# Self-attention in a decoder kernel: each value product cut into two halves of 256 columns, spread over its step

## What is computed

```python
# layer 0: 16 heads of width 16, causal
p = softmax(mask(q @ k.T * scale));  o = p @ v
# layer 1: 32 score heads of width 8; each pair of them shares one 16-wide value head
attn1 = softmax(q1 @ k1.T * scale) @ v12
attn2 = softmax(q2 @ k2.T * scale) @ v12
a = attn1 - lam * attn2          # then a root mean square norm and the output projection
```

## Time and profile before

| | |
|---|---|
| median of three runs | 4204.82 us (4199.30 to 4217.71) |
| profiled execution, its own time | 4222.62 us |
| its span, first to last instruction | 4220.9 us |
| TensorE busy | 3494.9 us (83%) |
| VectorE busy | 2918.8 us (69%) |
| ScalarE busy | 1941.5 us (46%) |
| GpSimd busy | 764.9 us (18%) |
| mean granted TensorE clock | 0.894 of 2.4 GHz |
| products (line 717) | 5632 records, 732.7 us busy, mean 593 ns |
| scores (line 701) | 2816 matmuls, 993.2 us busy |
| scores for the maxima (line 742) | 2816 matmuls, 1004.9 us busy |
| reductions (line 632) | 1408, 1561.4 us busy, 319.1 us idle before them |
| exponentials (line 569) | 2816, 1388.5 us busy, 567.7 us idle before them |

### The profile page before, as it was taken

The page is one execution under the profiler, slowest core; times in us unless marked ns, Lnnn a source line. Parts: engine busy times, 40 slices in busy tenths (PEclk is TensorE's granted clock), DMA queues, the critical chain, the costliest instruction groups (busy, mean ns, idle before and its releaser), DMA issues. The chain is left out here.

```text
span 4220.9 us, 54217 instructions
## 1 busy us (share of the span) xinstructions
PE 3494.9 (83%) x19000; PEld 1704.3 (40%) x19000; DVE 2918.8 (69%) x4353; ACT 1941.5 (46%) x3763; POOL 764.9 (18%) x1063
## 2 busy tenths in 40 slices
PE   7599999766479885999999999999865769999758
PEld 4244443433234452333333333333342434554625
DVE  6566665345546677888888888888645457776374
ACT  2166666222110031777777777777741213334121
POOL 3222222123300041000000000000022433445000
PEclk9689989688779995999999999999987879999678
DMA  5312210000010061000000000000001231110202
GB/s 201 111 44 50 48 44 20 18 35 10 0 41 10 10 198 53 17 24 17 17 24 16 23 18 17 24 16 17 9 3 38 98 104 42 32 32 1 88 17 71
DMA packets 81072, 175.16 MB, mean 41 GB/s; under 512 B 21592, under 2 KB 39008, under 8 KB 79424
## 3 DMA queue, kind: packets, MB, share of 16 engines
q1 hardware_dynamic: 79968, 165.76, 13.0%
q10 hardware_dynamic: 864, 6.29, 0.4%
HBM read 87.76 MB, written 54.72 MB: 34 GB/s over the span
## 5 line engine op out<-in xcount | busy, mean ns | idle before, releaser
L632 DVE TENSOR_REDUCE L_attn_tops<-L_attn_psM 128x2 f32<-128x1024 f32 (+3 forms) x1408 | 1561.4, 1148 | 319.1 <-PE L_attn_psM L742 315.7
L569 ACT ACTIVATE L_attn_E<-L_attn_psS 128x512 f32<-128x512 f32 (+3 forms) x2816 | 1388.5, 576 | 567.7 <-PE L_attn_psS L701 564.1
L701 PE MATMUL L_attn_psS<-L_attn_Q,L_attn_K 64*128 64x512 f32 (+3 forms) x2816 | 993.2, 437 | 126.1 <-ACT L_attn_E L569 101.8
L742 PE MATMUL L_attn_psM<-L_attn_K,L_attn_Q 62*128 62x512 f32 (+3 forms) x2816 | 1004.9, 479 | 55.8 <-DMA L_attn_K<-parts_k 30.3
L701 PEld LDWEIGHTS L_attn_psS<-L_attn_Q,L_attn_K 64*128 64x128 f32 x2816 | 470.1, 192 | 815.7 <-ACT L_attn_E L569 648.4
L717 PE MATMUL L_attn_psO<-L_attn_E,L_attn_V 128*32 128x512 f32 (+3 forms) x5632 | 732.7, 593 | 0.0
L742 PEld LDWEIGHTS L_attn_psM<-L_attn_K,L_attn_Q 62*128 62x128 f32 x2816 | 437.2, 193 | 149.2 <-issue 43.1
L527 POOL TENSOR_TENSOR L_AO<-L_attn_o 128x128 f32<-128x128 f32 x64 | 29.4, 459 | 1446.1 <-DVE L_attn_o L665 1446.1
L1437 PE MATMUL m_psE<-m_we,m_xT 128*128 128x512 f32 x512 | 236.9, 623 | 0.0
L536 POOL TENSOR_SCALAR_AFFINE_SELECT L_attn_E<-L_attn_E 128x128 f32<-128x128 f32 x512 | 146.2, 292 | 463.0 <-ACT L_attn_E L569 451.7
L2135 ACT ACTIVATE x_E<-x_psS 128x512 f32<-128x512 f32 x256 | 138.9, 595 | 179.8 <-PE x_psS L2258 167.1
(11 more groups left out here) (339 smaller groups left out, 3793.1 us busy)
## 6 DMA issues: line engine op xcount, KB each, us to landing
parts_q<-L_proj_parts SPq DMA_DIRECT2D x64, 256.0 KB
parts_k<-L_proj_parts SPq DMA_DIRECT2D x64, 256.0 KB
L_attn_Q<-parts_q SPq DMA_DIRECT2D x192, 64.0 KB
L_attn_K<-parts_k SPq DMA_DIRECT2D x192, 64.0 KB
L_attn_Q<-parts_q SPq DMA_DIRECT2D x64, 128.0 KB
L_attn_K<-parts_k SPq DMA_DIRECT2D x64, 128.0 KB
queries<-x1p_qo SPq DMA_DIRECT2D x16, 512.0 KB
keys<-x1p_ko SPq DMA_DIRECT2D x16, 512.0 KB
```

Source lines behind the costliest of these rows:

```text
L569: act.activation(E[(4 * n + s) % 8][:, c0:], psS[bank][:, c0:], ACT.Exp, scale=scale).then_inc(e_done, 1)
L632: dve.tensor_reduce(dst, src, AX, ALU.max).then_inc(m_read, 1)
L701: pe.matmul(psS[bank][:, c0:], K[g.slot][r:r + RH, c, kt * P:(kt + 1) * P], Q[g.slot][r:r + RH, c, q * HALF + c0:(q + 1) * HALF], start=Tr ...
L742: last = pe.matmul(psM[bank][:, j * HALF:j * HALF + n], Q[t.slot][r:r + TOP, c, qt * P:(qt + 1) * P], K[t.slot][r:r + TOP, c, h * HALF:h * ...
```

## The change

A product is cut in two. The first half covers columns 0 to 255 and is issued behind the scores of heads 0 and 1; the second covers columns 256 to 511 and is issued behind those of heads 2 and 3, where the whole product stood. On the diagonal only columns from c0 on exist: a product of 384 columns becomes 128 and 256, those of 256 and 128 columns have no first half. In layer 0 the product lags its scores by two steps instead of one, with twelve E buffers instead of eight; in layer 1 it still lags by one. `scored` counts ahead which exponential a product has to wait for. Evacuations, the first transposes of a turn (BACK1, from place 7 to place 8 in layer 0) and the starting value of o_done move along. ScalarE waits for a free E behind the wait for its first score, not ahead of it.

```diff
+    BACK = 2 if causal else 1
+    RING = BACK + 1
-    BACK1, BACK0 = LATE + 2, LATE + ends[0] + 3
+    BACK1, BACK0 = LATE + BACK + 1, LATE + ends[0] + BACK + (1 if causal else 2)
-        E = [m.sb(f"{tag}_attn_E{k}", [P, HALF]) for k in range(8)]
+        E = [m.sb(f"{tag}_attn_E{k}", [P, HALF]) for k in range(4 * RING)]
...
+        scored, count = {}, 0
+        for g in range(1, groups + 2):
+            for n in in_turn(g < groups, g <= groups):
+                at = (g - 1, n - LATE) if n >= LATE else (g - 2, NS + n - LATE)
+                if 0 <= at[0] < groups:
+                    scored[at] = count
+                    count += 4
+                if n == 0 and g <= groups:
+                    count += 1
...
-                    act.wait_ge(o_done, g.times(NS, n + 1))
                     for s in range(4):
                         i, bank = s_item(t, place + s)
                         act.wait_ge(s_done, i + 1)
+                        if s == 0:
+                            act.wait_ge(o_done, g.times(NS, n + 1))
...
-                        if old and k == 0:
+                        if old and k == BACK - 1:
                             evacuate(t + -2, 1)
-                        if last and k == ends[0] + 1:
+                        if last and k == ends[0] + BACK:
                             evacuate(t + -1, 0)
...
-                pe.sem_inc(o_done, 2)
+                pe.sem_inc(o_done, RING)
...
+                def product(at, n, half):
+                    g = At(at, None, 3)
                     q, kt, c0 = steps[n]
+                    lo, hi = max(c0, half * HALF // 2), (half + 1) * HALF // 2
+                    if lo >= hi:
+                        return
+                    if lo == c0:
+                        if n == 0 or steps[n - 1][0] != q:
+                            pe.wait_ge(o_out, g.times(2, q))
+                        if n == 0:
+                            pe.wait_ge(v_in, g.times(1, 1))
+                        if diagonal[n]:
+                            pe.wait_ge(e_cut, cuts(g, n + 1))
+                        else:
+                            pe.wait_ge(e_done, scored[at, n] + 4 + 3)
                     for s in range(4):
+                        last = pe.matmul(psO[32 * s:32 * s + 32, lo:hi], V[g.slot][:, kt, s // shared, :],
+                                         E[(4 * n + s) % (4 * RING)][:, lo:hi], start=(kt == 0 and half == 0), stop=(n == ends[q]),
                                          skip_group_check=True)
+                    if half == 1:
+                        last.then_inc(o_done, 1)
+
+                def products(t, n, last, old, half):
+                    j = n - LATE - BACK
+                    if j >= 0 and last:
+                        product(t.base - 1, j, half)
+                    if j < 0 and old:
+                        product(t.base - 2, NS + j, half)
...
+                            if s % 2 == 1:
+                                products(t, n, last, old, s // 2)
                         if last and n == 0:
                             turn_maxima(t, 4 if old else 0)
-                        if live and step >= 1:
-                            product(g, step - 1, s_item(t, place)[0] + 3)
-                        if old and k == 0:
-                            product(t + -2, NS - 1, s_item(t, s_place(LATE - 1, 3, last, old))[0] + 4)
```

More of the change, by code:

```diff
@@ L357, in attend @@
     LATE = 5
+    BACK = 2 if causal else 1
+    RING = BACK + 1
+    assert NS * 4 % (4 * RING) == 0 and BACK < LATE
     assert NP2 == 2 * NS
@@ L516, in copy @@
                     if g.base >= 3:
-                        pool.wait_ge(o_done, (g + -2).times(NS, 2))
+                        pool.wait_ge(o_done, (g + -2).times(NS, RING))
                     src = VA[:, g.span(), :, :]
@@ L533, in trim @@
                         pool.wait_ge(e_done, s_item(t, place + s)[0] + 4)
-                        block = E[(4 * n + s) % 8][:, c0:c0 + P]
+                        block = E[(4 * n + s) % (4 * RING)][:, c0:c0 + P]
                         pool.sem_inc(passed, 1)
@@ L568, in exps @@
                         act.wait_ge(s_done, i + 1)
-                        act.activation(E[(4 * n + s) % 8][:, c0:], psS[bank][:, c0:], ACT.Exp, scale=scale).then_inc(e_done, 1)
+                        if s == 0:
+                            act.wait_ge(o_done, g.times(NS, n + 1))
+                        act.activation(E[(4 * n + s) % (4 * RING)][:, c0:], psS[bank][:, c0:], ACT.Exp, scale=scale).then_inc(e_done, 1)
                 def maxima(t, place):
@@ L576, in evacuate @@
                 def evacuate(g, q):
-                    act.wait_ge(o_done, g.times(NS, 2 + ends[q] + 1))
+                    act.wait_ge(o_done, g.times(NS, RING + ends[q] + 1))
                     act.activation(oT[q][:], psO[:], ACT.Copy).then_inc(o_out, 1)
@@ L702, in score @@
                               Q[g.slot][r:r + RH, c, q * HALF + c0:(q + 1) * HALF], start=True, stop=True).then_inc(s_done, 1)
-                def product(g, n, done):
+                def product(at, n, half):
+                    g = At(at, None, 3)
                     q, kt, c0 = steps[n]
[L706 to L715, removed]
+                    lo, hi = max(c0, half * HALF // 2), (half + 1) * HALF // 2
[10 more added lines that the diff above has]
+                            pe.wait_ge(e_done, scored[at, n] + 4 + 3)
                     for s in range(4):
-                        last = pe.matmul(psO[32 * s:32 * s + 32, c0:HALF], V[g.slot][:, kt, s // shared, :],
-                                         E[(4 * n + s) % 8][:, c0:], start=(kt == 0), stop=(n == ends[q]),
+                        last = pe.matmul(psO[32 * s:32 * s + 32, lo:hi], V[g.slot][:, kt, s // shared, :],
+                                         E[(4 * n + s) % (4 * RING)][:, lo:hi], start=(kt == 0 and half == 0), stop=(n == ends[q]),
                                          skip_group_check=True)
-                    last.then_inc(o_done, 1)
+                    if half == 1:
[6 more added lines that the diff above has]
+                        product(t.base - 2, NS + j, half)
                 def turn_back(t, g, q, k):
```

## The result

The changed kernel took 4143.59 us in the median of four runs (4138.51 to 4160.97), the kernel before 4211.13 in the median of four: a ratio of 0.985 (interval 0.9819 to 0.9882). The profiled execution took 4145.7 us, 76.9 less than that of before. In a later batch four more runs of the changed kernel took 4151.6, 4153.98, 4228.14 and 4229.93 us. The last two are slower than any run of the kernel before in that batch (4193.69 to 4221.85); experiment 3 deals with them. A ratio here leaves out executions over 1.5% above the fastest of the same kernel, which medians and ranges include, so it isn't quite the quotient of two medians.

A forecast was written before the change was run, and what follows sets the result against it. Layer 1 bound by a closed chain through ScalarE and the whole product, layer 0 by TensorE; -46 - 5 + 33 - 27 = -45 against 4222.6 gives 4178, 40 off the 4204.8 median gives 4165 us; 4105 to 4225 holds 8 in 10.

The forecast's parts named there:

- The price of a half: TensorE, layer 1: cutting adds 0.15 us, one more change between scores and products 0.19; 0.34 a step in all.
- the step of layer 1: Layer 1: a step falls from 2.67 to 2.48 us, TensorE the longest, ahead of VectorE 2.36 and ScalarE's chain 2.31.
- the cheap cut: Rival: changes overlap, layer 1's step falls to its chains, 2.36 us; -110 us in all, 4095; chance 0.12.
- the dear cut: Slower rival: first half costs 0.45, exponentials late by 0.1, layer 1's step stays 2.67; +60 us, 4265; chance 0.10.
- What is late next: New waits per layer 1 group: evacuation +0.8, turn back +0.3, maxima 0.45 us; net gain 1.5 a group.
- Layer 0's fifteen groups: Layer 0: each group grows by 2.2 us at full clock, +33 over 15 groups; less half clock gives -27.
- The last turn of layer 0: Layer 0's last turn: no change, 0, between -5 and +5 us.
- The clock of layer 0: Layer 0: half clock follows the wait for the maxima's DMAs; without that wait 0.8 of 34 us goes, -27.
- The rival for the clock: Slower rival: layer 1's new 0.45 us wait brings half clock in one group of four, 4.9 us each; 4230; chance 0.10.
- the 34 us: Layer 0 before the change: excess of average over full-clock group time, 2.62 x 13, taken as time at half clock.
- The worth of layer 0's part: Layer 0: cut and lag cost +33 us over 15 groups, less half clock saves 27.

The follow-up runs named there:

- experiment 3: Reruns: the changed kernel again, 4151.6 to 4229.93 us; the kernel before with only layer 0's part of the change, 4329.68 us.
- experiment 4: The kernel before with only ScalarE's wait for a free E buffer moved behind its score wait, products whole: 4182.61 us, ratio 0.9946.

## Why the prediction came out as it did

The forecast was 4165 in a range of 4105 to 4225; the first four runs, median 4143.6, lie inside and on the side called likeliest. That none of them stayed long at half clock was luck: two of the next four lie above 4225. By its steps:

- **The price of a half and the step of layer 1** were right: 0.57, 0.33 and 0.34, 2.48 us, TensorE with no gap. The rule that the chains would bind at 2.36 (the cheap cut) is out; so is the dear cut, whose point was a step of 2.60. The Trainium skill (TensorEngine Tiling (Array Packing), Key Properties) says that a change of mode drains the engine; the trace agrees in that each change has a price, 0.14 us fixed to each part and 0.10 to each score between two parts; that the drain is what costs it, no run shows.
- **What is late next** was named rightly and sized too high: the evacuation costs 0.26 twice (0.4 forecast), the maxima 0.29 (0.45), the turn back 0.26 twice (0.15). Some of this was there before (1.69 beside the steps), so the waits add 1.0 a group and not 1.55. Net 2.0 and not 1.5: 42.49, not 43.0. Layer 1 gave 61.3 for 46, its last turn 8 for 5.
- **ScalarE's moved wait** was passed over in the sum. Alone it brings 44.41 - 43.64 = 0.77 us a group, about 25 us in all (experiment 4). The step of 2.48 stands all the same, since TensorE binds it; of the 2.0 a group, 0.77 can be had by the wait alone, and the cut adds 43.64 - 42.39 = 1.25 to it. The cut without the moved wait was not tried, so how the two share the step's 0.19 is not shown further.
- **Layer 0's fifteen groups**: +1.9 a group at full clock, +2.2 forecast. They take 528.1 us before and after in spite of 15 x 1.9 = 28, so the clock gave back 28, as the forecast's 27 had it.
- **The last turn of layer 0** was put at 0 (-5 to +5) and gave 13.3 us, all that layer 0 gained. The prediction looked for a gap ahead of head 3 in the groups alone; in this turn the same waits for an exponential stand (0.31 to 0.52 before, up to the fall of the clock), and with 17 to 23 us of half clock whole products take 48.8 to 51.2 us here, halves 44.5 to 46.3. By that comparison of profiles some 5 us are the form's, and the other 8 the length of half clock, which differs from profile to profile. That waits under 0.6 bring no half clock does not hold here.
- **The clock of layer 0** is the step that failed in kind. I took half clock as short stretches behind waits, which go when the waits go. In the middle of the layer that holds in the profiled run. But the layer starts at half clock in every profile, and the halved form can stay there for groups, or fall back and stay for 92 or 266 us, as the whole form did in no profile ahead of the last turn. The rival for the clock put this into layer 1, where halves leave it early. In the profiled run layer 0 gained 13 us; three groups of 57.7 take 70 away. (The price of 4.9 us in that rival is off too: the 34 us lie in six of the thirteen groups behind them, not in seven of fourteen, 5.7 each.)
- **The worth of layer 0's part**, +33 - 27, was near nothing. Alone, with the moved wait in it, it comes to 1.0014; the wait alone comes to 0.9946, so the part loses 0.7%, some 29 us (40 in the medians of all runs). What the prediction did not ask is whether the lag is worth having without the cut: it is, 4101 against 4144 (0.9758 against 0.985 of the kernel before beside them).

## What to carry to other kernels

A closed chain with one long block in it shortens when the block is cut, but only where the chain and not the engine sets the step; where the engine is full already (layer 0), each cut is its price and nothing else. Where a transfer is waited for once a group, start its consumers a place later before anything is cut. And look at the scatter of several runs and at the clock's row: a form that stays at half clock by chance can lose more in one stretch than the change gains in all.

## Of the hardware

- With TensorE busy at 96 to 100%, 1.2 GHz can last for hundreds of us. How long it did went with how fine the products were cut, as long as scores for the maxima ran beside them: ahead of layer 0's last turn at most 41 us behind the start in whole form, up to 266 in halves; in layer 1 under one group whole or halved, some 370 us in quarters (0.50 from 1662 to 2034). In the last turn of layer 0, without those scores, the long stretches are of the whole form. Why is not shown.
- A score of 512 columns between two products costs 0.43 us, one with a score on one side 0.33 or 0.34.
- On ScalarE the order of two waits ahead of an exponential, of which the score's is met last in both orders, was worth 0.06 us a time (0.54 and 0.60 from first score to first exponential).
